# Gathered message rows get a third block buffer, and three edge tiles move from the tensor engine to the gather engine

## What is computed

```
hr  = einsum('ni,rio->rno', x, weight)            # 3 relations, 512 nodes
msg = hr[edge_type, src] * edge_weight[:, None]    # 16896 edges
x   = layernorm(x + relu(segment_sum(msg, dst)))
```

## Time and profile before

| | |
|---|---|
| median of 3 runs | 592.39 us (590.75 to 593.99) |
| profiled execution, its own time | 590.65 us |
| its span, first to last instruction | 588.8 us |
| PE busy | 484.7 us, 82% |
| DVE busy | 398.2 us, 68% |
| ACT busy | 325.1 us, 55% |
| POOL busy | 303.4 us, 52% |
| mean granted TensorE clock | 0.956 of full |

### The profile page before, as it was taken

One profiled execution on the slowest core, in us unless ns is written; L12 is line 12 of the kernel. 1 busy time (PEld: TensorE's weight loads), 2 busy tenths in 40 slices (PEclk: granted clock), 3 DMA queues, 4 the chain that ended last, 5 costly groups with the idle time before them and its releaser, 6 DMA issues.

```text
span 588.8 us, 9670 instructions
## 1 busy us (share of the span) xinstructions
PE 484.7 (82%) x3463; PEld 346.7 (59%) x3463; DVE 398.2 (68%) x1114; ACT 325.1 (55%) x832; POOL 303.4 (52%) x320
## 2 busy tenths in 40 slices
PE   8439888988889899568988888888997489589896
PEld 4328666766667785346767676666874145244353
DVE  5228767777768795437877777676986169467585
ACT  3237655655656675245566566555774245446463
POOL 6752667466556303726664656665007556475510
PEclk9769999999999999779999999999999699998899
DMA  5852566566656404735664556666011111111100
GB/s 185 273 164 74 173 193 177 144 184 189 172 162 173 139 11 129 208 93 161 179 176 130 161 162 177 180 171 185 5 55 50 40 46 37 36 51 31 46 10 19
DMA packets 28346, 72.85 MB, mean 124 GB/s; under 512 B 6795, under 2 KB 10691, under 8 KB 28298
## 3 DMA queue, kind: packets, MB, share of 16 engines
q0 software_dynamic: 20768, 64.77, 38.6%
q1 hardware_dynamic: 6442, 6.54, 4.0%
q10 hardware_dynamic: 1088, 0.92, 0.5%
HBM read 69.05 MB, written 3.16 MB: 123 GB/s over the span
## 4 chain that ended last, share of the span: by engine, by line
PE 48%; DVE 17%; ACT 13%; another core or an unknown queue 12%; issue 11%; ACTq 0%; DVEq 0%
PE gates L1245 19%; PE gates L1238 5%; PE work L1492 5%; PE work L1245 3%; DVE prod_fc L897 3%; DVE prod_ig L899 3%; PE work L1478 2%; DVE h_full L868 2%; ACT h_hi L588 2%; PE gates L1168 2%; DVE msg_full L1081 2%; ACT act_if L592 2%; DVE h_lo L881 2%; ACT msg_full L741 2%
## 5 line engine op out<-in xcount | busy, mean ns | idle before, releaser
L519 POOL DMA_INDIRECT rows<-gate_table,src_steps x226 | 220.0, 973 | 177.1 <-PE gates L1245 70.9
L1245 PE MATMUL gates<-h_hi,whh_hi 128*128 128x256 f16 x396 | 102.9, 278 | 19.7 <-issue 12.0
L592 ACT ACTIVATE act_if<-gates 128x512 f32<-128x512 f32 x113 | 67.5, 598 | 89.4 <-PE gates L1245 45.2
L530 POOL DMA_INDIRECT edge_rows<-msg_table,msg_index x76 | 74.2, 976 | 80.0 <-ACT msg_full L741 31.9
L1238 PE MATMUL gates<-ident,rows 128*128 128x128 f32 x686 | 97.0, 276 | 22.0 <-issue 15.8
L1245 PE MATMUL gates<-h_hi,whh_lo 128*128 128x256 f16 x396 | 102.3, 277 | 0.7 <-issue 0.7
L897 DVE TENSOR_TENSOR prod_fc<-act_if,cell 128x256 f32<-128x256 f32 x128 | 54.0, 422 | 70.4 <-issue 37.3
L1238 PEld LDWEIGHTS gates<-ident,rows 128*128 128x128 f32 x686 | 77.5, 142 | 31.5 <-issue 29.6
L1245 PE MATMUL gates<-h_lo,whh_hi 128*128 128x256 f16 x396 | 86.7, 277 | 3.8 <-issue 3.8
L899 DVE TENSOR_TENSOR prod_ig<-act_if,act_g 128x256 f32<-128x256 f32 x128 | 53.8, 421 | 14.4 <-issue 11.4
L881 DVE TENSOR_TENSOR h_lo<-h_full,h_hi 128x256 f16<-128x256 f32 x128 | 54.0, 422 | 12.2 <-ACT h_hi L588 1.1
(11 more groups left out here) (186 smaller groups left out, 808.7 us busy)
## 6 DMA issues: line engine op xcount, KB each, us to landing
rows<-gate_table,src_steps POOLq DMA_INDIRECT x226
gate_table<-rows SPq DMA_DIRECT2D x8, 256.0 KB
edge_rows<-msg_table,msg_index POOLq DMA_INDIRECT x76
code<-code_table SPq DMA_DIRECT2D x6, 160.0 KB
msg_table<-table_sb SPq DMA_DIRECT2D x4, 192.0 KB, 2.4
code<-code_table SPq DMA_DIRECT2D x5, 128.0 KB
whhT<-turned_whh SPq DMA_DIRECT2D x2, 256.0 KB
wihT<-turned_wih ACTq DMA_DIRECT2D x1, 256.0 KB, 2.9
```

The source lines that it names most:

```text
L519: pool.indirect_dma_start(rows[:, j * K + k, :], None, gate_table[l], bass.IndirectOffsetOnAxis(src_steps[:, t, k:k + 1], axis=0)).then_in ...
L530: pool.indirect_dma_start(edge_rows[:, c % 2, n, :], None, msg_rows, bass.IndirectOffsetOnAxis(msg_index[:, pool_first(c) + n:pool_first(c ...
L592: act.activation(act_if[:, h, :], gates[:, h, 0, :], ACT.Sigmoid, scale=1 / G_SCALE).then_inc(if_ready[h], 1)
L1245: mm = pe.matmul(gate_place(t, h, gate), w[:, gate * P:(gate + 1) * P], state[:, h, :], start=(opens and opens_bank(t, gate) and n == 0), ...
```

## The change

`PE_TILES` is changed in blocks 3, 4, 5, 9 and 10 (5, 4, 5, 5, 5 tiles become 4, 5, 4, 4, 4): 53 tiles by PE, 79 gathered. The gathered tiles per block were 0, 7, 8, 7, 8, 7, 8, 7, 8, 7, 7, 2 and are 0, 7, 8, 8, 7, 8, 8, 7, 8, 8, 8, 2. Block buffers are chosen by c % 3: buffers 0 and 1 are those of `edge_rows`, buffer 2 is slots 12 and 13 of `rows`, with those slots' own semaphores, whose count starts from the fills that the LSTM made. POOL waits from block 4 on, for the tile three blocks earlier. ACT reads and waits at the new places.

```diff
-    PE_TILES = (6, 5, 4, 5, 4, 5, 4, 5, 4, 5, 5, 4)
+    PE_TILES = (6, 5, 4, 4, 5, 4, 4, 5, 4, 4, 4, 4)
-    assert C == P and len(PE_TILES) == BLOCKS and N == G and NM <= SLOTS
+    assert C == P and len(PE_TILES) == BLOCKS and N == G and NM + NG <= SLOTS
+        def edge_rows_of(c, n):
+            return edge_rows[:, c % 3, n, :] if c % 3 < 2 else rows[:, NM + n // 4, n % 4 * C:(n % 4 + 1) * C]
         def slot_fills(c, n):
-            return sum(SIZES[b] - PE_TILES[b] > n for b in range(c % 2, c + 1, 2))
+            return sum(SIZES[b] - PE_TILES[b] > n for b in range(c % 3, c + 1, 3))
+        def edge_rows_landed(c, n):
+            if c % 3 < 2:
+                return edge_rows_in[c % 3][n], 16 * slot_fills(c, n)
+            in_lstm = sum((NM + n) % K in gathered_tiles(t) for turn, (_, t) in enumerate(fetched)
+                          if turn % DEEP == (NM + n) // K)
+            return rows_in[NM + n], 16 * (in_lstm + slot_fills(c, n))
@@ POOL
-                    if c >= 3:
-                        pool.wait_ge(rows_taken, pool_first(c - 2) + min(n + 1, SIZES[c - 2] - PE_TILES[c - 2]))
+                    if c >= 4:
+                        pool.wait_ge(rows_taken, pool_first(c - 3) + min(n + 1, SIZES[c - 3] - PE_TILES[c - 3]))
                     pool.indirect_dma_start(
-                        edge_rows[:, c % 2, n, :], None, msg_rows,
+                        edge_rows_of(c, n), None, msg_rows,
...
-                        ).then_inc(edge_rows_in[c % 2][n], 16)
+                        ).then_inc(edge_rows_landed(c, n)[0], 16)
@@ ACT
-                        act.wait_ge(edge_rows_in[c % 2][n], 16 * slot_fills(c, n))
-                        act.activation(msg_full[:, k % 2, m, :], edge_rows[:, c % 2, n, :], ACT.Copy,
+                        act.wait_ge(*edge_rows_landed(c, n))
+                        act.activation(msg_full[:, k % 2, m, :], edge_rows_of(c, n), ACT.Copy,
```

## The result

The changed kernel took 598.53 us (median of 4 runs, 597.34 to 604.19), the kernel before beside it 593.19 us; the ratio is 1.012, interval 1.0075 to 1.0164. Every ratio leaves out executions that ran over 1.5% above the fastest of the same kernel (two of the 589.24 us set), so it can differ a little from that of the medians. The profiled execution took 598.91 us, its span 597.1 us, 8.3 us more than before. 2.2 us of these lie ahead of the relational part (first gather at 442.87 instead of 440.64). From the first gather to PE's last turn of the sums it is 148.2 us instead of 142.1: +6.1 us is what the part itself lost.

A forecast was written before the change was run, and what follows sets the result against it. The prediction took PE's signals, held during POOL's uninterrupted gathers, as the limit, and PE itself once gathers end. +10.0 − 2.8 − 1.8 + 1.5 = +6.9, taken as +6: 596.7 profiled, 597.5 us median; range 593 to 603, 8 in 10 585 to 603.

The forecast's parts named there:

- The first run and its end: Start of the relational part: first run grows from 19 to 27 gathers, ACT released at its end, 476 instead of 466: +10.0 us.
- theory of runs: Relational part: PE's signals get through for some 9 us of uninterrupted gathers, then hardly until POOL pauses; sum +6.9 us.
- Rival A: Wherever gathers stand, each costs 0.39 us, whatever the run's length: −1.6 us, no measurable change, 589 to 592; chance 0.19.
- Rival B: First stall stays 11 us, its end at POOL's pause a coincidence; gathers finish earlier: −7.5 us, 583 to 585; chance 0.24.
- the last stall: The stall at 548 to 554.7, which a rival said would lose its cause and vanish: −5.9 us.
- Rival C: From block 5 on POOL never pauses, each block waits for its gathers' end: +14 us, 605; chance 0.07.
- the earlier end of the gathers: Later blocks: gathers end one block earlier; a block costs 12.0 us with gathers, 9.2 without: −2.8 us.
- −1.8 for PE: Blocks 9 and 10, now free of gathers and bound by PE, have fewer tiles on PE: −1.8 us.
- three gathers more: One counted in the first run; two others cost 0.8 to 2.5 us, and runs pause less: +1.5 us taken.
- POOL waits for ACT changes little in total: Sign of being right: POOL's total wait for ACT to free row buffers, 31.9 us before, stays about the same.
- hardly at all until the run pauses: Relational part: after some 9 us of uninterrupted gathers, PE's signals hardly get through until POOL pauses.
- within 2 us of that run's end: Sign of being right: ACT's L723 that started at 466.09 starts this close to the end of the first run, near 474.

The follow-up runs named there:

- the repeat: The changed kernel run again without edit, beside the kernel before, on another chip with the stall: 601.26 against 593.53 us, 1.0109.
- two blocks only: Kernel before with 61 of 76 gathers left out, blocks 3 to 11 reading again what blocks 1 and 2 gathered: 569.48 against 589.24 us, 0.9683.
- The run with SP: Kernel before with POOL's 76 gathers replaced by plain DMAs of contiguous rows, same bytes, issued by SP: 558.29 against 589.24 us, 0.9507.

## Why the prediction was right, and where it was lucky

*The first run and its end.* The run has 27 gathers, as counted. ACT has the whole picked block, both halves, 35.3 us after the first gather, before 26.9: +8.4 (+11.1 in the repeat), forecast +10.0. All six traces with gathers and with the stall, in us after the first gather:

| kernel | gathers in the first run | run ends | first half copied | second half copied |
|---|---|---|---|---|
| 8 rows outstanding | 12 | 15.3 | 17.1 | 17.6 |
| two blocks only | 15 | 19.2 | 15.7 | 21.4 |
| before | 19 | 23.8 | 25.5 | 26.9 |
| third buffer alone | 26 | 32.8 | 19.9 | 32.5 |
| changed | 27 | 34.3 | 22.0 | 35.3 |
| changed, once more | 27 | 33.5 | 37.3 | 38.0 |

The second half moves with the run's end, from 0.3 us before it to 4.6 us behind, when the run is made shorter and longer by edit. That is the theory of runs, shown for the first run. The first half doesn't follow it: in three of the six it comes 3.4 to 12.9 us before the end. Rival A, the toll of 0.39 us a gather, would have moved the second half by 3 us over 8 gathers and 6 us over the table, where it moved by 8 to 11 and by 18 to 20: fallen for the first run. For the rest of the part it isn't excluded. In the changed kernel the three blocks with the run of 21 took 35.5 us (490.61 to 526.07, 23 gathers), the two with a run of 11 took 24.1 (526.07 to 550.13, 15 gathers); above 9.2 us a block that is 0.34 and 0.38 us lost per gather, so there the longer run cost no more. Rival B, that the release is a coincidence, has fallen with the same table, and the last stall, which it said would vanish, is there (3.90 us at 558.87). Rival C: no.

*What comes later* (−2.8 for the earlier end of the gathers, −1.8 for PE, +1.5 for three gathers more: −3.1): from the second half's copy to the last turn it was 115.2 us and is 112.9, −2.3 (−4.3 in the repeat). The three terms weren't measured apart.

*The sum* was +6.9, taken at +6; the part measured +6.1 and +6.8, the medians +5.3 and +7.7. That the sum fits better than its two terms is partly luck: in the first trace they are 1.6 and 0.8 us smaller in size than forecast, in the repeat 1.1 and 1.2 us larger, and as their signs differ the errors cancel in part.

*What failed:* "POOL waits for ACT changes little in total": it fell from 31.9 to 18.9 us. I had argued that the same pattern comes one block later. But the waits of the last blocks before (555.9 to 563.5, 7.6 us) have no match now: behind 550 POOL waits for ACT 0.3 us. And from 490.4 to 518.9 it doesn't wait for ACT once; that the blocks with 8 gathers keep POOL busier fits this but isn't shown. And "hardly at all until the run pauses" was too strict. A half got through in the middle of the first run in three kernels (at 464.85 in the changed one), and in the later run of 21 gathers all did, with waits of 2.94 us at most. Of the prediction's rows, too, two don't have the release behind the pause: 528.59 is 0.1 us before the end of the last gather of its run, and so is 552.57. Finally, "within 2 us of that run's end" held for the second half in the first trace (1.0) and not in the repeat (3.8 and 4.6).

*The weak point* is what the prediction took for granted, that the stall belongs to the kernel. It belongs to the kernel on some chips, and that the changed kernel was measured on such a chip is luck: no row foretold it. On the others the change itself wasn't run, but its two parts took 459 and 462 us there, where 597.5 was forecast for the whole. Where it is absent the buffer alone is worth nothing (1.000), the tiles cost 0.7%, and rival B's claim that gathers don't hold PE is simply true; the rule of the Trainium skill that was set against the forecast (Trainium Architecture — The Big Picture, What this means for kernel authors: DMA and engines don't contend at SBUF) is borne out there (PE busy 98.66 of 100.9 us beside the gathers). The run with SP agrees with it where the stall is, since the same traffic held nothing. Nothing in the profile of before could show that a second kind of chip exists.

*Open:* what joins POOL's indirect DMAs to ACT's late start, why on some chips only, why the first run is so much dearer than the later run of 21, and what is late: PE's work, its signal, or ACT itself. For the copy at 464.85 the profile names no wait at all ("issue"), so a cause on ACT's own side is a rival that no run tests.

## What to carry to other kernels

A wait of the producer for a free buffer is not a loss when nobody waits for its data; before adding a buffer, look for what the producer's pauses may be doing for others. When an unnamed stall ends again and again at the same event of another engine, count that event's runs: the length of the first run set the price here, and bounding the number of rows outstanding (8 instead of 15) gave 1.0% for a two-line edit on the chip with the stall. Look for the run that breaks the rule as well, which here is the one of 21 gathers. And time a change on more than one chip before a fine tuning of who does what: the third buffer costs 2.0% on one kind and nothing on the other, and what the three tiles do is known on one kind alone.

## What the runs showed of the hardware that I had not expected

The same program takes 458 to 459 us on two chips and 589 to 594 us on others, where PE is busy 97% against 81 to 82% of the time. On the latter, while POOL issues its first run of indirect DMAs back to back, ACT starts a copy up to 16.5 us after it has nothing else to do, though the matmuls it needs are recorded as done long before; 76 plain DMAs of the same size from SP, at 50 GB/s, delay none. On the former a run of 76 indirect DMAs delays none either. POOL itself is as fast on both: 1.25 us from start to start (median), 1.3 us on average, since some of the gathers take longer.
